# First tiles of a mixture of experts from two groups' counts, rows of 1216 bytes, and list scatters tied to other engines

## The chip, the cores and the metric

One core of one Trainium2 chip runs the whole kernel in one launch. The metric is device time in microseconds (us) of that core; the kernel before takes 544.88 us, the median of three runs (544.68 to 546.29).

## The reference, cut to what matters

```python
# x, ctx: (16, 128, 256).  16 batches of 128 tokens = 2048 tokens of 256 values
x = x + tanh(g_xattn) * xattn(ctx, ctx, layernorm(x))    # long convolution of k*v pairs, times q
x = x + tanh(g_ffn) * ffn(layernorm(x))

def ffn(x):                                   # 32 experts, 6 chosen for each token
    scores = sigmoid(xf @ w_router)           # (2048, 32)
    topk_idx = top 6 of (scores + corr_bias) within the 4 best of 8 expert groups
    combine[t, e] = scores[t, e] for the 6 chosen experts, else 0
    eo = (silu(xf @ gate_w[e]) * (xf @ up_w[e])) @ down_w[e]      # 256 -> 176 -> 256
    routed = sum over e of combine[:, e] * eo[e]
    shared = (silu(xf @ sh_gate_w) * (xf @ sh_up_w)) @ sh_down_w
    return routed + shared
```

## The kernel before, in words

The sixteen batches are worked in four groups of four (`GB = 4`, `NG = 4`). Each of the four groups goes through attention, layer norm, router, choice of experts and the shared expert; `group(g, attend, route)` exists once for each engine, and one call routes group g while it makes the attention products of group g + 1. The call for the last group (g = 3, `attend` False) has no attention products to make and builds the tile tables instead.

**Lists.** Every expert owns a list of 2048 rows in device memory (`expert_lists`), first filled with blank rows from SBUF. A row is `ROW = 289` floats: 256 normalised values, the token's number (`TOK_AT`), and its 32 router scores (`SCORE_AT:ROW`). Once VectorE has the slots of a group (`slots_ready`, L765), GpSimd sends 24 indirect DMAs (L395), one for each of 4 batches and 6 choices, each with 128 rows, at most `AHEAD = 6` of them unlanded. After 24 it waits until all have landed and raises `payload_free` (L400). SBUF holds the rows of two groups: `payload` for the even groups and `payload_2` for the odd ones.

**Tiles.** A tile is 128 rows of one expert's list. SyncE loads it (L313), TensorE transposes it (`xT`, L1196), multiplies it with the gate and up weights (`gate_up`, L1207), transposes the hidden values (`hT`, L1217) and multiplies with the down weights (`down`, L1226). VectorE copies x out (L973), picks the weight of each row (`pick`, L978 to L985) and multiplies up with silu (L991). ScalarE does the silu (L554), a copy (L561) and the scaled copy of y (L569) into one of 16 buffers. GpSimd adds y to `token_sums` with an indirect DMA (`add_tile`, L410); an add waits until the add two tiles before has landed, and its first one comes, in GpSimd's program, behind all 96 list scatters. The first program order on TensorE is xT(t), gate_up(t - 1), hT(t - 2), down(t - 3). There are 96 sure tiles and then blocks of four as the counts need; this input takes 108.

**The early table.** The first `NA = 16` tiles are full ones whose rows are known before the last group is routed. `describe_known` makes their table from `count_a`, the counts of the first `KNOWN = 12` batches (three groups), over the first `EA = 18` experts. VectorE copies the counts at group 2 (L757); the table is ready at L877 (`tables_a_ready`). The other tiles come from the whole counts (`describe_tiles`), ready at L951 (`tables_ready`). SyncE loads tiles into the four blocks of `payload`, `NX = 4` tiles ahead, so it first waits for `payload_free` to reach 4: the scatters of groups 0 to 2, of which groups 0 and 2 read `payload`.

**Weights.** The arena in SBUF holds all expert weights in the tile phase, and before that the attention's buffers; an expert's weights can be loaded once what lies there is dead. Up weights of the 14 first experts come early (L255 on SyncE). Behind `pairs_summed` 8, SyncE issues the down weights of experts 0 to 17 and the up weights of 14 to 17; ScalarE issues the up weights of 18 to 31 in one DMA after the scores of group 3, and behind `tables_ready` the down weights of 18 to 31 in two. TensorE waits for ScalarE's three DMAs (`last_in`) before tile 16.

**The end.** When all adds have landed, SyncE reads the two copies of `token_sums` back (L342), VectorE adds them to x (L1013, L1015) and the result is stored.

Of the kernel before, what the change touches and what calls it, by code (L numbers as in the profile page):

```python
# [9 lines left out]
GB = 4  # L10
# [17 lines left out]
ROW = L + 1 + E  # L28
TOK_AT, SCORE_AT = L, L + 1
# [30 lines left out]
assert ROUTER_AT + KC * E <= ARENA  # L60
# [3 lines left out]
WD_LAST = (X2T_AT - WD_AT) // WD_E // 2 * 2  # L64
assert WD_AT <= TMP_AT
# [13 lines left out]
assert TE_AT + NTILES <= WORK and NX <= GB  # L79

# [6 lines left out]
KNOWN = (NG - 1) * GB  # L87
EA = WD_MID
# [3 lines left out]
def build(nc, x, ctx_t, toeplitz, g_xattn, g_ffn, skip_d, w_router, corr_bias,  # L92
# [10 lines left out]
    with ctx:  # L103
# [18 lines left out]
        y_rows = sb("y_rows", [P, 3, L])  # L122
# [115 lines left out]
        y_at = [(y_rows, i * L) for i in range(3)] + [(blank, 0)]  # L238
        y_at += [(b, i * L) for b in (q_sb, shgu_sb, shd_sb) for i in range(4)]
        y_row = lambda t: win(*y_at[t % YR], [[1, L]])  # L240
        pick_w = lambda t: win(work, TW_AT + t % NPICK, [[1, 1]])
# [31 lines left out]
        def _(sp):  # L273
# [34 lines left out]
            def load_tile(t):  # L308
# [4 lines left out]
                sp.dma_start(payload[:, t % NX, :], lists[bass.ds(first, P), :]).then_inc(t_loaded[t % NX], 16)  # L313
# [38 lines left out]
        def _(pool):  # L352
# [25 lines left out]
            link(nc.gpsimd.tensor_scalar(tok_id[:, :], win(lane_dump, 0, [[0, B]]), float(B), None, ALU.mult))  # L378
            link(nc.gpsimd.tensor_tensor(tok_id[:, :], tok_id[:, :], iota_e[:, 0:B], ALU.add))
# [51 lines left out]
        def _(act):  # L431
# [18 lines left out]
            def group(g, attend, route):  # L450
# [51 lines left out]
                if route:  # L502
# [17 lines left out]
                    nc.scalar.activation(pay[g % 2][:, :, SCORE_AT:ROW], win(bank[4], 0, [[E, GB], [1, E]]),  # L520
                                         ACT.Sigmoid).then_inc(scores_ready, 1)
# [775 lines left out]
```

## Time and profile before

| what | value |
|---|---|
| median of three runs | 544.88 us |
| profiled execution: its own time, its span | 550.49 us, 548.6 us |
| TensorE busy, of the span | 445.5 us (81%) |
| VectorE, ScalarE, GpSimd busy | 312.8, 203.9, 288.6 us |
| mean granted TensorE clock | 0.903 of full speed |
| DMA traffic | 85.38 MB |

The span is the part that the profiler shows; 1.9 us of the execution's own time lie around it. Start times are in us from the span's start. "Busy" adds up instructions, so it says nothing of what the end waited for: that is read from the chain of waits and from the order of time. A releaser named "issue", "remote" or "unknown queue" is time for which the trace has no cause.

### The profile page before, as it was taken

Reading aid. Unit: us, or ns where it says so; the run is one execution under the profiler, and the core shown is the slowest. Engines: PE = TensorE matmul, PEld = TensorE weight load, DVE = VectorE, ACT = ScalarE, POOL = GpSimd, SP = SyncE. Lnnn points to the kernel's source line nnn. Section 1 sums busy time; section 2 is a strip of 40 time slices with the busy share of each in tenths; the row PEclk is TensorE's granted clock in tenths of the full one; section 3 lists DMA queues with packets and bytes.
Section 4 is the critical chain, followed back from the end, with each engine's and each line's share of the span. In section 5 each row is a group of like instructions: output and inputs, shape, how many; then the busy total and the mean of one; then the engine's idle time right before and its main releaser. Section 6 shows DMA issues by size and latency. Waiting matters only on the chain.

```text
span 548.6 us, 8656 instructions
## 1 busy us (share of the span) xinstructions
PE 445.5 (81%) x2114; PEld 334.4 (61%) x2114; DVE 312.8 (57%) x1163; ACT 203.9 (37%) x522; POOL 288.6 (53%) x224
## 2 busy tenths in 40 slices
PE   0924989798888668646999999999999999999900
PEld 0724767666766456424777777777777777777700
DVE  3999999859968755303444444444444444444307
ACT  3531725533462322002444444444444444444400
POOL 2000038848884752771556566665656566656630
PEclk9985989989988959755999999999999999999965
DMA  7999302222221499983666666566656665666569
GB/s 260 357 302 404 156 32 84 97 87 101 90 98 55 146 257 340 357 292 106 108 116 107 118 110 121 108 118 106 121 108 118 107 121 106 119 108 122 67 145 351
DMA packets 56053, 85.38 MB, mean 156 GB/s; under 512 B 6492, under 2 KB 47676, under 8 KB 55740
## 3 DMA queue, kind: packets, MB, share of 16 engines
q1 hardware_dynamic: 33566, 46.68, 28.8%
q0 software_dynamic: 20160, 28.37, 26.7%
q10 hardware_dynamic: 2270, 9.68, 4.6%
q8 instruction: 23, 0.38, 0.3%
q14 instruction: 34, 0.28, 0.2%
HBM read 44.91 MB, written 39.80 MB: 154 GB/s over the span
## 4 chain that ended last, share of the span: by engine, by line
PE 61%; DVE 22%; issue 7%; DMA 4%; ACT 2%; another core or an unknown queue 2%; SPq 1%; POOL 1%; DVEq 0%; POOLq 0%; ACTq 0%
PE bank L1207 24%; PE bank L1226 17%; DVE arena L658 5%; PE bank L1196 5%; PE bank L1217 4%; PE bank L1069 3%; DVE arena L636 3%; PE bank L1090 3%; DVE arena L666 3%; DMA arena<-token_sums 2%; DVE arena L615 1%; DMA rows<-x 1%; PE bank L1079 1%; PE bank L1040 1%
## 5 line engine op out<-in xcount | busy, mean ns | idle before, releaser
L395 POOL DMA_INDIRECT expert_lists<-payload,slots x96 | 116.7, 1216 | 126.3 <-DVE slots L765 84.3
L1207 PE MATMUL bank<-wgu,work 128*128 x432 | 149.8, 470 | 6.8 <-issue 5.2
L1226 PE MATMUL bank<-wd,work 88*128 x432 | 111.9, 382 | 0.0
L991 DVE TENSOR_TENSOR work<-work,bank 128x176 f32<-128x176 f32 x108 | 36.4, 337 | 128.2 <-ACT work L554 113.6
L1207 PEld LDWEIGHTS bank<-wgu,work 128*128 128x128 f32 x432 | 75.2, 194 | 31.8 <-issue 9.5
L554 ACT ACTIVATE work<-bank 128x176 f32<-128x176 f32 x108 | 34.2, 317 | 125.5 <-PE bank L1207 96.9
L1226 PEld LDWEIGHTS bank<-wd,work 88*128 88x128 f32 x432 | 73.9, 191 | 6.2 <-issue 0.2
L973 DVE COPY work<-bank 128x256 f32<-128x256 f32 x108 | 45.8, 424 | 34.4 <-PE bank L1196 18.6
L410 POOL DMA_INDIRECT token_sums<-q_sb,dest x28 | 43.6, 1558 | 27.2 <-ACT q_sb L569 7.3
L410 POOL DMA_INDIRECT token_sums<-shgu_sb,dest x28 | 43.6, 1559 | 24.8 <-DMA token_sums<-shgu_sb,dest 6.8
L1217 PEld LDWEIGHTS bank<-ident,work 128*88 128x88 f32 x216 | 26.5, 123 | 37.7 <-issue 18.8
L410 POOL DMA_INDIRECT token_sums<-shd_sb,dest x24 | 37.4, 1558 | 22.2 <-DVE work L985 7.7
L410 POOL DMA_INDIRECT token_sums<-y_rows,dest x21 | 32.8, 1561 | 29.7 <-ACT y_rows L569 15.3
L1217 PE MATMUL bank<-ident,work 128*88 128x128 f32 x216 | 41.8, 275 | 6.6 <-DVE work L991 6.6
L1040 PE MATMUL bank<-arena 128*128 128x288 f32 x128 | 45.8, 442 | 1.5 <-DVE arena L643 1.0
L1069 PE MATMUL bank<-shgu_sb,arena 128*128 128x352 f32 x128 | 46.5, 512 | 0.0
L658 DVE TENSOR_TENSOR arena<-arena,q_sb 128x448 f32<-128x448 f32 (+7 forms) x120 | 45.4, 454 | 0.0
L1196 PE MATMUL bank<-ident,payload 128*128 128x128 f32 x216 | 42.8, 280 | 0.7 <-issue 0.7
L561 ACT COPY work<-bank 88x256 f32<-88x256 f32 x108 | 39.7, 367 | 0.1
L1196 PEld LDWEIGHTS bank<-ident,payload 128*128 128x128 f32 x216 | 31.3, 146 | 12.6 <-issue 2.1
L457 ACT COPY arena<-bank 128x288 f32<-128x288 f32 x64 | 25.3, 399 | 26.7 <-PE bank L1041 23.4
L1069 PEld LDWEIGHTS bank<-shgu_sb,arena 128*128 128x128 f32 x128 | 26.2, 216 | 12.5 <-issue 4.0
(170 smaller groups left out, 570.1 us busy)
## 6 DMA issues: line engine op xcount, KB each, us to landing
payload<-expert_lists SPq DMA_DIRECT2D x108, 144.5 KB
wgu<-w_gu SPq DMA_DIRECT2D x1, 4928.0 KB, 19.1
wgu<-w_gu ACTq DMA_DIRECT2D x1, 4928.0 KB
expert_lists<-blank SPq DMA_DIRECT2D x1, 4768.5 KB, 25.4
arena<-token_sums SPq DMA_DIRECT2D x8, 512.0 KB, 7.3
wd<-w_down SPq DMA_DIRECT2D x1, 3168.0 KB
token_sums<-blank SPq DMA_DIRECT2D x1, 2304.0 KB, 28.9
arena<-toeplitz ACTq DMA_DIRECT2D x2, 1024.0 KB, 10.5
```

The source lines that it names most:

```text
L395: nc.gpsimd.indirect_dma_start(lists, bass.IndirectOffsetOnAxis(ap=slots[:, g % 2, b, k:k + 1], axis=0), pay[g % 2][:, b, :], None).then_i ...
L410: nc.gpsimd.indirect_dma_start(sums, bass.IndirectOffsetOnAxis(ap=dest[:, t % NPICK:t % NPICK + 1], axis=0), y_row(t), None, compute_op=AL ...
L561: nc.scalar.copy(win(work, HT_AT + t % 2 * L, [[1, L]], parts=MH), bank[4 + t % 2][0:MH, 0:L]).then_inc(t_hT_copied, 1)
L658: last = nc.vector.tensor_tensor(win(arena, Z_AT + z0, [[DH * DH, CELLS], [1, DH - d]]), y, win(q_sb, q_at + i0, [[DH, CELLS], [1, DH - d] ...
L973: nc.vector.tensor_copy(win(work, XT_AT + t % 2 * L, [[1, L]]), bank[t % 2][:, 0:L]).then_inc(t_x, 1)
L991: nc.vector.tensor_tensor(win(work, H_AT + t % 2 * M, [[1, M]]), win(work, SG_AT + t % 2 * M, [[1, M]]), bank[2 + t % 2][:, M:2 * M], ALU. ...
L1040: nc.tensor.matmul(y[:, 0:2 * CB], toe(h, 0), prods(s, hh, 0, 2), start=True, stop=False)
L1069: last = nc.tensor.matmul(bank[5 + half][:, 0:SHM], x2T(b, k), shgu_sb[:, k, half * SHM:(half + 1) * SHM], start=(k == 0), stop=(k == KC - 1))
L1196: last = nc.tensor.transpose(bank[t % 2][:, k * P:(k + 1) * P], payload[:, t % NX, k * P:(k + 1) * P], ident[:, :])
L1207: last = nc.tensor.matmul(bank[2 + t % 2][:, 0:2 * M], xT_half(t, k), wgu[:, bass.ds(e * WGU_E + k * 2 * M, 2 * M)], start=(k == 0), stop= ...
L1217: last = nc.tensor.transpose(bank[4 + t % 2][0:MH, c * P:(c + 1) * P], win(work, H_AT + t % 2 * M + c * MH, [[1, MH]]), ident[:, :])
L1226: last = nc.tensor.matmul(bank[6 + t % 2][:, 0:L], hT_half(t, c), wd[:, bass.ds(e * WD_E + c * L, L)], start=(c == 0), stop=(c == 1))
```

## The change

* `KNOWN` falls from 12 to 8 batches and `EA` from 18 to 14 experts; the early counts are taken at group 1 instead of group 2.
* A row grows from 289 to 304 floats (1156 to 1216 bytes); GpSimd sets the new tail to zero once.
* Tiles 0 to 7 (`IN_ARENA`) go to four blocks of their own in the arena, and SyncE loads them behind `payload_free` 3 (groups 0 and 1) and the early table; later tiles go to `payload` as before, behind `payload_free` 4.
* SyncE's late DMA is only the down weights of experts 0 to 13. All other weights come from ScalarE in 18 DMAs of two experts each: up weights in the last group's stage (six) and behind the steps of tiles 0 to 2 (three), down weights behind the steps of tiles 0 to 8.
* GpSimd waits before list scatters for counts of other engines. TensorE waits for 18 DMAs before tile 16.
* One y buffer moves from `y_rows` to `shgu_sb`; there are still 16.

```diff
-ROW = L + 1 + E
-TOK_AT, SCORE_AT = L, L + 1
+ROW = -(-(L + 1 + E) // 16) * 16
+TOK_AT, SCORE_AT, SCORE_END = L, L + 1, L + 1 + E
...
+TILES_AT = ROUTER_AT + KC * E
+assert TILES_AT + 4 * ROW <= ARENA
...
+WD_TILES = (ROUTER_AT - WD_AT) // WD_E // 2 * 2
+LATE = [n for n in range(EARLY, E, 2)]
...
+IN_ARENA = 2 * NX
-KNOWN = (NG - 1) * GB
-EA = WD_MID
+KNOWN = (NG - 2) * GB
+EA = EARLY
...
+        tile_rows = lambda t, at, n: (win(arena, TILES_AT + t % NX * ROW + at, [[1, n]]) if t < IN_ARENA
+                                      else payload[:, t % NX, at:at + n])
...
             sp.wait_ge(pairs_summed, 2 * NG)
-            load_down(sp, 0, WD_MID, late_in)
-            load_up(sp, EARLY, WD_MID, late_in)
+            load_down(sp, 0, EARLY, late_in)
+            sp.wait_ge(payload_free, NG - 1)
             sp.wait_ge(tables_a_ready, 1)
+            for t in range(IN_ARENA):
+                load_tile(t)
             sp.wait_ge(payload_free, NG)
-            for t in range(NX):
-                load_tile(t)
-            for t in range(NX, NA):
+            for t in range(IN_ARENA, NA):
                 load_tile(t)
...
+            for p in pay:
+                nc.gpsimd.memset(p[:, :, SCORE_END:ROW], 0.0)
...
+                        nth_of = b * TOPK + k
+                        if g == NG - 1 and 0 < nth_of < GB * TOPK // 2:
+                            pool.wait_ge(sh_h_ready, g * GB + 1 + nth_of // 3)
+                        elif g == NG - 2 and nth_of >= GB * TOPK // 2:
+                            pool.wait_ge(attn_ready, (g + 1) * 2 + 1)
+                            if nth_of >= GB * TOPK * 3 // 4:
+                                pool.wait_ge(x2T_ready, (g + 1) * 2 + 1)
+                        elif g < NG - 2 and nth_of >= GB * TOPK // 2:
+                            pool.wait_ge(conv_copied, (g + 2) * NH + 1 + (nth_of - GB * TOPK // 2) // 2)
+                        elif g == NG - 1 and nth_of:
+                            pool.wait_ge(t_xT, 1 + (nth_of - GB * TOPK // 2) // 2)
...
+                    if not attend:                                  # ACT, after the x2T copies
+                        act.wait_ge(pairs_summed, 2 * NG)
+                        load_up(act, EARLY, EARLY + 2, last_in)
...
                     if not attend:                                  # ACT, after the scores
-                        load_up(act, WD_MID, E, last_in)
+                        load_up(act, EARLY + 2, EARLY + 4, last_in)
...
+                        if not attend:                              # ACT, in the shared expert's loop over b
+                            load_up(act, EARLY + 4 + 2 * b, EARLY + 6 + 2 * b, last_in)
...
+            def late_weights(t):
+                if t < 3:
+                    n = EARLY + 12 + 2 * t
+                    load_up(act, n, n + 2, last_in)
+                if t < len(LATE):
+                    n = LATE[t]
+                    if n == WD_LAST:
+                        act.wait_ge(sh_stored, 16 * (B - GB))
+                        act.wait_ge(sh_added, GB)
+                    if n == WD_TILES:
+                        act.wait_ge(t_xT, IN_ARENA)
+                        act.wait_ge(t_picked, IN_ARENA)
+                    load_down(act, n, n + 2, last_in)
             act.wait_ge(tables_ready, 1)
-            load_down(act, WD_MID, WD_LAST, last_in)
-            act.wait_ge(sh_stored, 16 * (B - GB))
-            act.wait_ge(sh_added, GB)
-            load_down(act, WD_LAST, E, last_in)
...
+                if t < NA:                                          # ACT, last in tile_step(t)
+                    late_weights(t)
...
-                    if g == NG - 2:                                 # DVE and PE: the early counts
+                    if g == NG - 3:
...
-                    pe.wait_ge(last_in, 48)
+                    pe.wait_ge(last_in, 2 * len(LATE) * 16)
```

(The comments are added here. Where a kernel line read `payload[:, t % NX, ...]` for a tile, it now calls `tile_rows`, and `SCORE_AT:ROW` is now `SCORE_AT:SCORE_END`.)

## Rows read from the trace of the kernel before

**Rows 1.** The page's chain that ended last, share of the span by engine

```profile
PE 61%; DVE 22%; issue 7%; DMA 4%; ACT 2%; another core or an unknown queue 2%; SPq 1%; POOL 1%; DVEq 0%; POOLq 0%; ACTq 0%
```

**Rows 2.** The stretch of the tile loop: busy time by engine, clock, DMA share, GB/s

```profile
262.00:512.00 250.00, 250.00 (x1207) 185.28 (x1206) 115.60 (x505) 106.36 (x302) 155.68 (x101) 1.00 0.64 113
```

**Rows 3.** TensorE in order of time: start, length, line, operation, idle before

```profile
230.27 0.63 PE L1196 MATMUL bank<-ident,payload 128*128 128x128 f32 x2
235.68 2.71 PE L1207 MATMUL bank<-wgu,work 128*128 x4 [3.42 <-issue]
...
257.62 1.47 PE L1207 MATMUL bank<-wgu,work 128*128 x4
260.00 0.38 PE L1196 MATMUL bank<-ident,payload 128*128 128x128 f32 x2
262.72 1.35 PE L1207 MATMUL bank<-wgu,work 128*128 x4
...
516.53 1.35 PE L1207 MATMUL bank<-wgu,work 128*128 x4
```

**Rows 4.** The same table of busy times, three stretches around the tile loop's start

```profile
220.00:224.00 4.00, 3.59 (x19) 2.76 (x17) 2.08 (x11) 0.46 (x1) 3.06 (x4) 1.00 1.03 410
...
244.00:248.00 4.00, 0.00 (x0) 0.00 (x0) 0.00 (x0) 0.00 (x0) 3.08 (x4) 0.50 0.80 279
...
252.00:256.00 4.00, 3.45 (x8) 2.21 (x9) 1.80 (x8) 1.16 (x4) 0.00 (x0) 0.50 0.25 70
```

**Rows 5.** Who waited for whom, 226 to 262 us: total, times, longest

```profile
ACT work L554 <- issue: 22.3, 1, 22.3
```

**Rows 6.** GpSimd in order of time: last scatters of group 2, group 3's, first adds

```profile
206.81 0.96 POOL L395 DMA_INDIRECT expert_lists<-payload,slots  x1 [0.30 <-issue]
217.96 0.96 POOL L395 DMA_INDIRECT expert_lists<-payload,slots  x1 [10.19 <-issue]
247.04 0.96 POOL L395 DMA_INDIRECT expert_lists<-payload,slots  x1 [0.30 <-issue]
258.75 1.61 POOL L410 DMA_INDIRECT token_sums<-y_rows,dest  x1 [10.75 <-ACT y_rows L569]
```

**Rows 7.** GpSimd's read of the block count, just behind the last landing

```profile
L215 POOLq TENSOR_LOAD <-tile_code x1: 512/512/512, 252.4 to 252.4; - x1
```

**Rows 8.** GpSimd's adds, first and last of two stretches of 6 and 12

```profile
359.69 1.56 POOL L410 DMA_INDIRECT token_sums<-shgu_sb,dest  x1 [1.27 <-DMA token_sums<-q_sb,dest]
371.72 1.56 POOL L410 DMA_INDIRECT token_sums<-shd_sb,dest  x1 [1.00 <-DMA token_sums<-shgu_sb,dest]
...
489.26 1.56 POOL L410 DMA_INDIRECT token_sums<-shd_sb,dest  x1 [1.66 <-DMA token_sums<-shgu_sb,dest]
516.16 1.56 POOL L410 DMA_INDIRECT token_sums<-q_sb,dest  x1 [0.94 <-DMA token_sums<-q_sb,dest]
```

**Rows 9.** The chain's end in order of time: start, length, what

```profile
520.09 0.48 ACT shgu_sb L569
...
525.38 3.58 DMA token_sums<-shgu_sb,dest
```

**Rows 10.** VectorE in order of time, in the last group's stage

```profile
198.16 0.19 DVE L860 TENSOR_TENSOR taken_a<-arena 128x32 f32<-128x32 f32 x1 [1.82 <-remote]
```

**Rows 11.** DMA issues, 180 to 262 us: count, KB each

```profile
wgu<-w_gu ACTq DMA_DIRECT2D x1, 4928.0 KB
wd<-w_down SPq DMA_DIRECT2D x1, 3168.0 KB
wgu<-w_gu SPq DMA_DIRECT2D x1, 1408.0 KB
...
payload<-expert_lists SPq DMA_DIRECT2D x9, 144.5 KB
```

**Rows 12.** GpSimd in order of time, a long scatter of group 0

```profile
91.42 4.13 POOL L395 DMA_INDIRECT expert_lists<-payload,slots  x1 [0.30 <-issue]
```

**Rows 13.** ScalarE's issue of its up weights, in order of time

```profile
205.95 0.39 ACTq L255 DMA_DIRECT2D wgu<-w_gu  x1
```

More of the change, by code:

```diff
@@ L59 @@
 ROUTER_AT = SHOUT_AT + 2 * L
-assert ROUTER_AT + KC * E <= ARENA
+TILES_AT = ROUTER_AT + KC * E
+assert TILES_AT + 4 * ROW <= ARENA
 STATS_AT, MOMENTS_AT, NEWTON_AT = TMP_AT, TMP_AT + 6 * B, TMP_AT + 8 * B
@@ L121, in build @@
         payload_2 = sb("payload_2", [P, GB, ROW])
-        y_rows = sb("y_rows", [P, 3, L])
+        y_rows = sb("y_rows", [P, 2, L])
         blank = sb("blank", [P, ROW])
@@ L237, in build @@
         hT_half = lambda t, c: win(work, HT_AT + t % 2 * L + c * P, [[1, P]], parts=MH)
-        y_at = [(y_rows, i * L) for i in range(3)] + [(blank, 0)]
-        y_at += [(b, i * L) for b in (q_sb, shgu_sb, shd_sb) for i in range(4)]
+        y_at = [(y_rows, i * L) for i in range(2)] + [(blank, 0)]
+        y_at += [(b, i * L) for b, n in ((q_sb, 4), (shgu_sb, 5), (shd_sb, 4)) for i in range(n)]
         y_row = lambda t: win(*y_at[t % YR], [[1, L]])
+        tile_rows = lambda t, at, n: (win(arena, TILES_AT + t % NX * ROW + at, [[1, n]]) if t < IN_ARENA
+                                      else payload[:, t % NX, at:at + n])
         pick_w = lambda t: win(work, TW_AT + t % NPICK, [[1, 1]])
@@ L312, in load_tile @@
                 first = table_value(sp, tile_row, t, E * LIST)
-                sp.dma_start(payload[:, t % NX, :], lists[bass.ds(first, P), :]).then_inc(t_loaded[t % NX], 16)
+                sp.dma_start(tile_rows(t, 0, ROW), lists[bass.ds(first, P), :]).then_inc(t_loaded[t % NX], 16)
             def load_block(n):
@@ L519, in group @@
                     act.wait_ge(logits_ready, g + 1)
-                    nc.scalar.activation(pay[g % 2][:, :, SCORE_AT:ROW], win(bank[4], 0, [[E, GB], [1, E]]),
+                    nc.scalar.activation(pay[g % 2][:, :, SCORE_AT:SCORE_END], win(bank[4], 0, [[E, GB], [1, E]]),
                                          ACT.Sigmoid).then_inc(scores_ready, 1)
@@ L708, in flat @@
                         return win(arena, o, [[step, n]])
-                    scores = pay[g % 2][:, :, SCORE_AT:ROW]
+                    scores = pay[g % 2][:, :, SCORE_AT:SCORE_END]
                     sfc = tmp(GB, E)
@@ L977, in pick @@
                 mask = win(work, MASK_AT + t % 2 * E, [[1, E]])
-                nc.vector.scalar_tensor_tensor(mask, iota_e[:, :], tile_e[:, t:t + 1], payload[:, t % NX, SCORE_AT:ROW],
+                nc.vector.scalar_tensor_tensor(mask, iota_e[:, :], tile_e[:, t:t + 1], tile_rows(t, SCORE_AT, E),
                                                ALU.is_equal, ALU.mult).then_inc(t_masked, 1)
@@ L981, in pick @@
                     dve.wait_ge(t_added[t % NX], nth(t - NPICK))
-                nc.vector.tensor_scalar(dest[:, t % NPICK:t % NPICK + 1], payload[:, t % NX, TOK_AT:TOK_AT + 1],
+                nc.vector.tensor_scalar(dest[:, t % NPICK:t % NPICK + 1], tile_rows(t, TOK_AT, 1),
                                         tile_dump[:, t:t + 1], float(t % S * SUM_ROWS), ALU.max, ALU.add)
@@ L1148, in group @@
                                             start=False, stop=True)
-                    if g == NG - 2:
+                    if g == NG - 3:
                         for seen in range(KNOWN):
@@ L1196, in xT @@
                     last = nc.tensor.transpose(bank[t % 2][:, k * P:(k + 1) * P],
-                                               payload[:, t % NX, k * P:(k + 1) * P], ident[:, :])
+                                               tile_rows(t, k * P, P), ident[:, :])
                 last.then_inc(t_xT, 1)
@@ L1253, in _ @@
             pe.wait_ge(early_in, 16)
-            pe.wait_ge(late_in, 32)
+            pe.wait_ge(late_in, 16)
             last = last_block(pe)
```

## The prediction

> **What bounds the kernel now.** I read the chain first: TensorE holds 61% of the span and VectorE 22% [rows 1]. The order of time splits this in three. Up to about 188 us VectorE's attention arithmetic sets the pace. From 257.6 us the tile loop runs: between 262 and 512 us TensorE is busy without a gap at full clock [rows 2], and gate_up goes from tile 5 at 262.72 to tile 107 at 516.53 [rows 3], which is 253.81 / 102 = 2.488 us a tile. Between the two lies the loop's start, and there nothing is busy: the first transposes stand at 230.27 us, yet gate_up(3) comes at 257.62 [rows 3], and from 244 to 248 TensorE, VectorE and ScalarE do nothing while the DMA engines are 80% busy and the clock granted is half, 1.2 GHz [rows 4]. ScalarE starts silu(0) only at the end of a 22.3 us gap with no cause shown [rows 5]. The DMA share falls from 0.80 to 0.25 just as the work resumes [rows 4].
>
> A second chain runs beside TensorE and is hidden by its busy row: GpSimd's adds. Group 3's first list scatter is held until 217.96 by the landing of group 2's, the last goes at 247.04, and the first add at 258.75 [rows 6]. Where GpSimd didn't wait for y, 5 gaps take 12.03 us and 11 gaps 26.90 us [rows 8]: 38.93 / 16 = 2.433 us an add. So an add isn't made much faster than a tile (2.488), and adds that start late stay late. That is what I take to set the end after the change: last ScalarE copy at 520.09, last add landed 3.58 us after 525.38, and only then can the sums come back [rows 9].
>
> **The change, part by part.**
>
> *Number of tiles.* Routing the reference's inputs gives 107 tiles over all experts, so 108 run. Over two groups the first 14 experts have 6, 6 and 5 full tiles at experts 0, 1 and 11: 17, which fills the 16 early tiles. No blank tile is added, and the loop keeps 108 steps. Had it been fewer than 16, each missing one would cost 2.49 us.
>
> *Early counts.* Twelve small bf16 matmuls leave group 2 and eight join group 1, a few tenths of a us each way: 0.
>
> *Last group's stage, 188 to 230 us.* SyncE's burst at 188 us falls from 3168 + 1408 KB [rows 11] to 14/18 of 3168, which is 2464 KB, and ScalarE adds 704 KB pieces (two experts of the 14 that make 4928 KB). Just before the loop the DMA engines were full with 410 GB/s [rows 4]; fewer bytes are now in flight. VectorE had a 1.82 us hole at 198.16 on its path, waiting for its own semaphore [rows 10]. I take this 1.8 us as gone; bounds 0 (it isn't the bytes) and 3. The six issues on ScalarE cost 0.39 us each [rows 13] and lie beside TensorE's shared-expert matmuls: 0; without that cover 2.3 us.
>
> *Loop's start.* Tiles 0 to 3 load at the early table instead of behind group 2's landing, and nearly all of the queued weight bytes ahead of them are gone. Ten us of that landing wait [rows 6] fall out of the path of the loads. In an undisturbed start gate_up(0) would come 1.8 us earlier than 235.68, at 233.9. Behind it stand gate_up(1) and (2), each 2.71 us on the low clock [rows 3], five transposes of 0.63 and the first down: some 10 us, so gate_up(3) would come at about 244, 13.6 us earlier than 257.62. New load: three up and nine down pieces, 3 x 704 + 9 x 352 = 5280 KB, in the steps of tiles 0 to 8. At the 410 GB/s seen at best here [rows 4] that is 13 us of all DMA engines inside some 22 us, beside two scatters a tile. So I keep 2 us of the holes: 11.6 us earlier, the 1.8 us included. Bounds: 0 (the same holes, moved) and 15. Then xT(5), at 260.00 [rows 3], comes at 248.4.
>
> *Scatters of group 3.* Twelve are tied to the shared expert and the last twelve to t_xT 1 to 6, two a tile. Two take 2 x 1.26 us (pitch of the rows' 0.96 + 0.30 [rows 6]), so GpSimd keeps up, and the last ends at 248.4 + 2.5 = 250.9. Behind it in GpSimd's program stand the landing wait and every add. From the end of the last scatter before (248.0) to the count's read at 252.4 [rows 7] is 4.4 us; with 1.3 us for the read and the first issue, the first add comes at 256.6 instead of 258.75: 2.1 us earlier. Bounds: 10 later (TensorE starts no earlier and the ties hold) and 6 earlier.
>
> *The adds.* 11.6 - 2.1 = 9.5 us more backlog than before, about 4 tiles, within the 16 y buffers. The adds catch up at 2.488 - 2.433 = 0.055 us each, 107 x 0.055 = 5.9 us. Bounds: 0, and the whole 9.5 us.
>
> *Ties of groups 0 to 2.* The waits on convolution copies and on group 3's attention are, by the order of the program, met about when GpSimd gets to the second half of a group, since long scatters (4.13 us [rows 12] against 0.96) already hold it back beside VectorE's work. 0, bounds -2 (fewer collisions with VectorE's choice of experts) and +2 (a scatter held past the next group's need of `payload`).
>
> *Rows of 1216 bytes.* 5% more bytes in list loads and scatters, in a loop where the DMA share is 0.64 [rows 2]: 0, bounds -1 and +1. The Trainium skill, "DMA: Bandwidth & Descriptors", section "How a descriptor splits into AXI transactions", says that a transfer starting off a 256-byte boundary fetches unused bytes; 1216 is still no multiple of 256, so by it most rows stay misaligned, and no row of this trace prices it.
>
> *Late weights on ScalarE.* Two issues of about 0.4 us [rows 13] in steps 0 to 2, one in 3 to 8, beside 106.36 us busy in 250 [rows 2], 1.06 us in a tile of 2.49: hidden. TensorE's wait before tile 16 comes 40 us after the start, against 13 us of transfer: hidden; if not, a rival below.
>
> **Sum.** First add 2.1 us earlier, catching up 5.9: 8.0 us. The profiled execution took 550.49 us (548.6 span and 1.9 around it), 5.6 above the median of 544.88, so I subtract from each: 542.5 for it, 536.9 for the median; I say 537.
>
> **Rivals.**
>
> *A, the adds catch up (or GpSimd starts sooner).* If the landing wait is shorter in a quieter queue and an add takes 2.35 us when it never waits for y, the backlog is gone by the end, and TensorE's 11.6 to 15 us come through: 530 to 533. For it: the add's own 1.56 us leaves room in 2.433 [rows 8]. Against it: those are the gaps seen when landings alone held it. I say 532.
>
> *B, the ties and the adds eat all.* The loop starts earlier, the first add doesn't, and the pace is the tiles': no change, 544 to 546. For it: the first add came 11 us behind the last scatter [rows 6].
>
> *C, slower: the weights starve the loop.* 5280 KB in the steps 0 to 8 share the DMA engines with the tile loads, each of which needs its own 144.5 KB [rows 11] within a tile. The 80% busy stretch moved 279 GB/s [rows 4]; at this rate weights, twelve scatters and nine loads (5.4 + 1.9 + 1.4 MB) take 31 us, against 22 of nine tiles, and each queue gets only a share. If tiles 2 to 8 come at 5 us instead of 2.49, 17.5 us go, the twenty-fourth scatter waits with them, and the first add stands at about 268: 9 us later than before, 5 of them made up: 549. It decides from the point where a tile load takes over 2.5 us, three tiles in a row. The Trainium skill, "DMA: Bandwidth & Descriptors", section "Queues, rings and completion order", says that each DMA engine goes round the queues packet by packet; by this rule the tile loads' small packets stand one for one behind weight packets several times as long, and C's starved loads would be the rule. The trace agrees in so far as GpSimd's last scatters of group 2 took 10.19 us to land beside the weights [rows 6].
>
> **Chances.** Forecast (533 to 541) 0.48; A 0.24; B 0.15; C 0.13. About 0.3%, 1.6 us, is what a measurement tells here. B lies half within it and a quarter on each side, C is slower: faster 0.76, same 0.10, slower 0.14. The range that leaves out 2 in 10: 529 to 545. The forecast's own: 533 to 541.
>
> **What would show it.** Right: gate_up(3) near 246, silu(0) within 3 us of gate_up(0); the first add near 256 and at least 8 us behind the first y; adds released by DMA landings or by nothing nearly all through; a wider gap than 5 us between the last TensorE work and the last add. Wrong: adds waiting for y again by mid-loop (A); holes of TensorE in tiles 2 to 8 behind tile loads, or a wait before tile 16 (C); a first add at 258 or later (B).

## The result: 1.1% slower

| | before | after |
|---|---|---|
| median, same chip | 545.59 us (4 runs, 544.68 to 547.89) | 553.15 us (4 runs, 551.79 to 555.41) |
| profiled execution | 550.49 us, span 548.6 | 555.41 us, span 553.5 |
| gate_up(0), (3), (107) | 235.68, 257.62, 516.53 | 237.22, 244.86, 509.40 |
| group 3's scatters, first and last | 217.96, 247.04 | 214.76, 252.28 |
| adds 0, 4 and 107 | 258.75, 268.95, 525.38 | 261.07, 275.19, 530.25 |
| last ScalarE copy of y (the one at 520.09 in [rows 9] is the last but one) | 521.03 | 513.90 |

The ratio is 1.0112, with a 95% interval of 1.0069 to 1.0155; the quotient of the two medians, 1.0139, lies in it. In some executions of a kernel the chip is in a slower state: the ratios leave these out, the medians do not. TensorE's last gate_up comes 7.1 us earlier and the last add 4.9 us later. The span follows the add: 553.5 - 548.6 = 4.9.

After, the chain that ended last (answers to [rows 1]). VectorE fell from 22 to 14%, DMA rose from 4 to 11%:

```profile
PE 61%; DVE 14%; DMA 11%; issue 6%; ACT 3%; another core or an unknown queue 2%; POOL 1%; SPq 1%; DVEq 0%; POOLq 0%; ACTq 0%
```

After, TensorE in order of time (start, length, line, operation, idle before; answers to [rows 3]):

```profile
237.22 2.71 PE L1244 MATMUL bank<-wgu,work 128*128 x4 [1.26 <-DVE work L1010]
240.15 1.95 PE L1244 MATMUL bank<-wgu,work 128*128 x4
...
242.37 1.35 PE L1244 MATMUL bank<-wgu,work 128*128 x4
...
244.86 1.35 PE L1244 MATMUL bank<-wgu,work 128*128 x4
...
249.33 1.35 PE L1244 MATMUL bank<-wgu,work 128*128 x4
...
253.53 0.44 PE L1233 MATMUL bank<-ident,arena 128*128 128x128 f32 x2 [1.77 <-DMA arena<-expert_lists]
253.83 1.58 PE L1244 MATMUL bank<-wgu,work 128*128 x4
...
257.76 1.68 PE L1244 MATMUL bank<-wgu,work 128*128 x4
...
260.59 1.35 PE L1244 MATMUL bank<-wgu,work 128*128 x4
...
509.40 1.35 PE L1244 MATMUL bank<-wgu,work 128*128 x4
```

These are gate_up(0) to (7), and (107). gate_up(3) is 12.8 us earlier. Then come four tiles in 15.73 us instead of 4 x 2.488 = 9.95, one of them held openly by a tile load (the transpose at 253.53). So 5.8 us are lost again. From gate_up(7) on the pace is 2.488 once more: (509.40 - 260.59) / 100.

After, busy time by engine in two stretches (answers to [rows 4]; columns PE, PEld, DVE, ACT, POOL, granted clock, DMA share, GB/s):

```profile
244.00:248.00 4.00, 2.63 (x12) 1.47 (x10) 0.98 (x5) 0.68 (x3) 1.83 (x2) 1.00 0.99 322
252.00:256.00 4.00, 2.47 (x9) 1.75 (x10) 0.63 (x2) 0.92 (x3) 0.96 (x1) 0.88 0.95 337
```

Where before nothing ran on the three engines and the clock stood at 1.2 GHz (0.50), they work in the first stretch at 2.4 GHz (1.00). But from 252 to 256 us, where the DMA engines were 25% busy, they are now 95% busy.

After, GpSimd in order of time (answers to [rows 6, 8]):

```profile
214.76 0.96 POOL L414 DMA_INDIRECT expert_lists<-payload,slots  x1 [8.02 <-DVE arena L721]
...
236.31 0.96 POOL L414 DMA_INDIRECT expert_lists<-payload,slots  x1 [2.54 <-PE bank L1233]
...
252.28 0.96 POOL L414 DMA_INDIRECT expert_lists<-payload,slots  x1 [0.30 <-issue]
261.07 1.61 POOL L429 DMA_INDIRECT token_sums<-y_rows,dest  x1 [7.83 <-ACT q_sb L604]
262.99 1.58 POOL L429 DMA_INDIRECT token_sums<-y_rows,dest  x1 [0.30 <-issue]
269.72 1.56 POOL L429 DMA_INDIRECT token_sums<-blank,dest  x1 [5.14 <-DMA token_sums<-y_rows,dest]
272.25 1.56 POOL L429 DMA_INDIRECT token_sums<-q_sb,dest  x1 [0.97 <-DMA token_sums<-y_rows,dest]
275.19 1.56 POOL L429 DMA_INDIRECT token_sums<-q_sb,dest  x1 [1.38 <-DMA token_sums<-blank,dest]
...
285.02 1.56 POOL L429 DMA_INDIRECT token_sums<-shgu_sb,dest  x1 [0.84 <-DMA token_sums<-q_sb,dest]
288.46 1.57 POOL L429 DMA_INDIRECT token_sums<-shgu_sb,dest  x1 [1.89 <-ACT shd_sb L604]
...
530.25 1.56 POOL L429 DMA_INDIRECT token_sums<-shgu_sb,dest  x1 [1.13 <-DMA token_sums<-shgu_sb,dest]
```

After, ScalarE's last copy of y (answers to [rows 9]):

```profile
513.90 0.47 ACT L604 ACTIVATE shgu_sb<-bank,work 128x256 f32<-128x256 f32 x1 [0.47 <-PE bank L1263]
```

Three readings. The tied scatters end at 253.24, 5.2 us later than before. The first add follows 7.83 us behind; its releaser is named as ScalarE's copy, but the first y was written at 247.91, so the landings of the scatters held it (the run with the landing wait moved, below, shows it: there the first add follows the last scatter within 0.3 us). And the last add starts 16.35 us behind the last y: the adds don't wait for tiles any more. Against before, the last add is later by +2.32 (first add), +3.92 (first four gaps: 14.12 us instead of 10.20) and -1.37 (103 gaps: 255.06 instead of 256.43) = +4.87 us.

### The profile page after: what moved, and what is told of

It reads as the page before. It is cut to its first block, busy times and chain, and to the rows that moved or that the text cites. A ratio compares the mean times of both kernels' runs of the same rounds, so it can differ in the third digit from the quotient of the medians.

```text
span 553.5 us, 8724 instructions
## 1 busy us (share of the span) xinstructions
PE 446.7 (81%) x2110; PEld 337.3 (61%) x2110; DVE 312.6 (56%) x1163; ACT 204.3 (37%) x522; POOL 289.2 (52%) x226
## 3 DMA queue, kind: packets, MB, share of 16 engines
q1 hardware_dynamic: 33118, 45.60, 27.2%
## 4 chain that ended last, share of the span: by engine, by line
PE 61%; DVE 14%; DMA 11%; issue 6%; ACT 3%; another core or an unknown queue 2%; POOL 1%; SPq 1%; DVEq 0%; POOLq 0%; ACTq 0%
PE bank L1244 20%; PE bank L1263 14%; PE bank L1106 6%; PE bank L1127 4%; PE bank L1233 4%; PE bank L1254 4%; DVE arena L695 4%; DMA token_sums<-shgu_sb,dest 4%; PE bank L1077 3%; DVE arena L703 2%; DMA arena<-token_sums 2%; PE bank L1078 2%; DMA arena<-expert_lists 2%; PE bank L1116 1%
## 5 line engine op out<-in xcount | busy, mean ns | idle before, releaser
L1244 PE MATMUL bank<-wgu,work 128*128 x432 | 148.1, 466 | 1.3 <-DVE work L1010 1.3
L429 POOL DMA_INDIRECT token_sums<-shgu_sb,dest x35 | 54.6, 1559 | 31.8 <-DMA token_sums<-shgu_sb,dest 10.7
L1106 PE MATMUL bank<-shgu_sb,arena 128*128 128x352 f32 x128 | 48.3, 527 | 0.0
L1233 PE MATMUL bank<-ident,payload 128*128 128x128 f32 x200 | 38.3, 272 | 0.0
L1233 PEld LDWEIGHTS bank<-ident,payload 128*128 128x128 f32 x200 | 28.4, 142 | 10.1 <-DMA payload<-expert_lists 0.2
L1127 PE MATMUL bank<-shd_sb,arena 88*128 88x256 f32 x128 | 32.3, 397 | 1.3 <-issue 0.7
```

Source lines behind the costliest of these rows:

```text
L429: nc.gpsimd.indirect_dma_start(sums, bass.IndirectOffsetOnAxis(ap=dest[:, t % NPICK:t % NPICK + 1], axis=0), y_row(t), None, compute_op=AL ...
L1106: last = nc.tensor.matmul(bank[5 + half][:, 0:SHM], x2T(b, k), shgu_sb[:, k, half * SHM:(half + 1) * SHM], start=(k == 0), stop=(k == KC - 1))
L1127: last = nc.tensor.matmul(bank[4][:, 0:L], win(arena, HST_AT + c * P, [[1, P]], parts=MH), shd_sb[0:MH, c, :], start=(c == 0), stop=(c == 3))
L1233: last = nc.tensor.transpose(bank[t % 2][:, k * P:(k + 1) * P], tile_rows(t, k * P, P), ident[:, :])
L1244: last = nc.tensor.matmul(bank[2 + t % 2][:, 0:2 * M], xT_half(t, k), wgu[:, bass.ds(e * WGU_E + k * 2 * M, 2 * M)], start=(k == 0), stop= ...
```

## The experiments

Ratios are to the kernel before on the same chip, with the 95% interval. The edits are shortened. The chips were not alike. Before took 536.9 and 537.9 us on two of them and 545.6, 547.9, 549.1 and 549.6 on the other four. Before itself was traced on two of the slower ones only, so the chips can be compared by the traces of all kernels together. Between 95 and 260 us, VectorE, ScalarE and TensorE's matmuls have next to no waits that the profile can't explain ("issue" and "remote") on the two quick chips, at most 1.2 us in all; on the other four, ScalarE has 22 to 58 us of them, VectorE 7 to 32 and TensorE 2 to 22. The quoted expectations were written before this was known.

### On a quick chip: the parts one by one (before 536.9 us)

**Group 3's ties left out.**

```
-if g == NG - 1 and 0 < nth_of < GB * TOPK // 2: wait sh_h_ready
-elif g == NG - 1 and nth_of: wait t_xT
```

> The changed kernel without the waits of group 3's list scatters on sh_h_ready and t_xT; the ties of groups 0 to 2 stay. Theory T (the adds on GpSimd set the end, and they start late because group 3's scatters are tied to the tiles): 24 scatters from about 215 at 1.27 us each end at 245 instead of 253, the first add comes near 253 instead of 261, the pace stays about 2.48, and the time falls by 7 to 9 us to 544 to 546. Rival W (the weight pieces on ScalarE's queue beside tiles 0 to 8 slow landings and loads, whoever goes first): the first add comes earlier, but the scatters collide with the weights, landings get longer, and the time stays within 3 us of 553. Rival R (rows of 1216 bytes): no change, 553.

541.04 us, 1.0068 [1.0035, 1.0100]. Last scatter 238.28, first add 246.36, last y 493.75, last add 516.13. TensorE in order of time:

```profile
216.60 2.71 PE L1240 MATMUL bank<-wgu,work 128*128 x4 [1.53 <-DVE work L1006]
...
223.83 1.35 PE L1240 MATMUL bank<-wgu,work 128*128 x4
```

The loop starts without a standstill although GpSimd has no ties: 7.2 us from gate_up(0) to (3), against 21.9 in [rows 3]. Still the kernel is slower than before.

**Ties of groups 0 to 2 left out.**

```
-elif g == NG - 2 and nth_of >= 12: wait attn_ready, x2T_ready
-elif g < NG - 2 and nth_of >= 12: wait conv_copied
```

> The changed kernel without the waits of the scatters of groups 0 to 2; group 3's stay. Theory T: nothing, within 2 us of 553, because the trace of the changed kernel has these scatters at the same starts as before up to 0.3 us. Rival E (the early ties delay group 2's landing or the last group's stage): 2 us or more faster, with VectorE's choice of experts in groups 1 to 3 earlier.

539.12 us, 1.0054 [1.0024, 1.0085]. Last scatter 238.22, first add 245.78, last 515.19.

**Rows of 1156 bytes as before.**

```
-ROW = -(-(L + 1 + E) // 16) * 16
+ROW = L + 1 + E
```

> The changed kernel with rows of 289 floats (1156 bytes) again, nothing else. Theory T: within 2 us of 553. Rival R (longer rows cost DMA time in scatters, loads and landings): 3 us or more faster, with the DMA share of the tile loop down from 0.65 and the pace of the adds below 2.47.

539.96 us, 1.0049 [1.0017, 1.0082]. Last scatter 240.25, first add 248.44, last 514.63. Neither the early ties nor the longer rows show: three kernels with different parts of the change taken out agree within their intervals. The whole change wasn't timed on this chip, so that is as far as it goes.

**Landing wait moved.** All ties are kept. Group 3's scatters are waited for behind the fourth add and no longer ahead of the first.

```
-for landed in scattered: pool.wait_ge(...); pool.sem_inc(payload_free)
+if g < NG - 1: scatters_landed(g)
...
+if t == 4: scatters_landed(NG - 1)     # in the loop of adds
```

> The changed kernel, ties kept, with GpSimd's wait for the landing of group 3's scatters (and its signal to SyncE) moved from ahead of the first add to behind the fourth. Theory T: the first add comes right behind the last scatter, near 255 instead of 261, and the time falls by 4 to 6 us to 547 to 549. Rival W: the first adds start at 255 but land as slowly as the weights let them (6 to 8 us for each pair), the fifth add comes near 270 to 275 as it does now (275.19), and the time falls by less than 2 us.

534.23 us, 0.9957 [0.9939, 0.9976]: faster than before, and 1% below its three neighbours, although it keeps everything that each of them leaves out. Last scatter 239.67, first add 240.95, fifth 255.90, last 510.15. Against those neighbours the first add is 4.8 to 7.5 us earlier and the last 4.5 to 6.0. So on this chip the adds' chain ends the changed kernel.

### The weights and a third sum (before 549.12 us)

**Before once more**, for its trace.

> The kernel before, unchanged, for a trace of the chip on which the three kernels beside it run. Theory T (GpSimd's adds set the end of the changed kernel): here the first add still follows the first y within 10 us, and the last add follows the last y within 6 us, on this chip too. The rival that the chips differ only by a factor would have every stage scaled alike.

550.75 us in one execution. gate_up(0) to (3) at 238.28, 244.57, 251.93, 256.66: the slow start is there again. ScalarE waits 23.4 us in one piece, named "remote". gate_up(0), whose result it needs, ends at 240.99, and ScalarE starts at 250.31: 9.3 us of the piece are without a cause. In the other trace of before it is 10.8 us (238.39 to 249.15).

**The changed kernel once more.**

> The changed kernel, unchanged, beside the kernel before on one chip. Both theories: slower than before by 0.3 to 1.2%. Theory T: the last gate_up comes 10 us or more earlier than in the kernel before, the first add not, and the last add stands more than 15 us behind the last y.

555.98 us, 1.0116 [1.0071, 1.0161]. gate_up(3) 244.11, last y 513.82. GpSimd in order of time:

```profile
252.29 0.96 POOL L414 DMA_INDIRECT expert_lists<-payload,slots  x1 [0.30 <-issue]
261.00 1.61 POOL L429 DMA_INDIRECT token_sums<-y_rows,dest  x1 [7.75 <-ACT q_sb L604]
...
267.63 1.56 POOL L429 DMA_INDIRECT token_sums<-blank,dest  x1 [3.12 <-DMA token_sums<-y_rows,dest]
...
528.85 1.56 POOL L429 DMA_INDIRECT token_sums<-shgu_sb,dest  x1 [0.82 <-DMA token_sums<-shgu_sb,dest]
```

**ScalarE's weights in bulk**, the ties kept: most in the stage, four experts at tile step 7, nothing in the steps 0 to 6.

```
-load_up / load_down of two experts behind each of the steps 0 to 8
+load_up(act, EARLY, E)               # behind the scores
+load_down(act, EARLY, WD_TILES)      # behind tables_ready
+if t == 7: load_down(act, WD_TILES, E)
```

> The changed kernel with ScalarE's weights in bulk, as before: the up weights of experts 14 to 31 in one DMA behind the scores, the down weights of 14 to 27 in two behind the tables, 28 to 31 at tile step 7. Ties, early tiles and rows stay. Theory T: TensorE's first tiles come later (3 to 10 us, since loads stand beside the bulk), which doesn't matter, and the time changes by the first add's time alone: -3 to +3 us. Rival W (the pieces beside tiles 0 to 8 slow the adds' landings): the first five adds come at 2.5 us each instead of 3.3 or more, and the time falls by 3 to 6 us.

550.96 us, 1.0048 [1.0017, 1.0079]. gate_up(3) is unchanged at 244.44. GpSimd:

```profile
252.36 0.96 POOL L414 DMA_INDIRECT expert_lists<-payload,slots  x1 [0.30 <-issue]
256.78 1.61 POOL L429 DMA_INDIRECT token_sums<-y_rows,dest  x1 [3.46 <-DVE work L1015]
...
261.39 1.56 POOL L429 DMA_INDIRECT token_sums<-blank,dest  x1 [1.11 <-DMA token_sums<-y_rows,dest]
...
270.41 1.56 POOL L429 DMA_INDIRECT token_sums<-q_sb,dest  x1 [5.43 <-DMA token_sums<-blank,dest]
```

The last scatter goes at the same time, and its landing wait falls from 7.75 to 3.46 us. The last add comes 4.3 us earlier (524.57). So the late pieces cost 4.2 us through the landing wait alone. By the Trainium skill, "DMA: Bandwidth & Descriptors", section "Queues, rings and completion order", a DMA engine goes round the queues that have work, packet by packet, which would make each packet of a scatter stand behind a weight packet. These two traces agree (7.75 and 3.46 us).

The first four gaps of the adds did not shrink to 2.5 us each as rival W has it: they take 13.6 us together, against 12.4 in the changed kernel beside it. 6.98 us of that is one gap, from the add at 263.43 to the one at 270.41, held by a landing. It stands beside the one late piece that is left, four experts issued at 261.55; the DMA share is 0.93 from 264 to 268 us.

**A third sum**: adds go in turn to three copies of `token_sums`, so an add waits for the one three tiles before.

```
-S = 2
+S = 3          # and one more add of 128x1024 per chunk at the end
```

> The changed kernel with three copies of token_sums instead of two (S = 3), so an add waits for the landing of the one three before it. It costs one more copy to blank, to read back (2 MB, some 5 us at the 9.84 us that two took) and to add. Theory T: the adds, free of the landing, go at about 2 us until they have caught up, the last add comes within 6 us of the last y, 15 us or more earlier than in the changed kernel, and the time falls by 8 to 13 us. Rival P (TensorE's tile loop or GpSimd's own issue time sets the end): the last add moves by less than 3 us and the time rises by 3 to 5.

548.92 us, 0.9989 [0.9962, 1.0016]. GpSimd, then ScalarE:

```profile
514.41 1.56 POOL L429 DMA_INDIRECT token_sums<-shgu_sb,dest  x1 [0.71 <-issue]
...
518.13 1.56 POOL L429 DMA_INDIRECT token_sums<-shgu_sb,dest  x1 [0.30 <-issue]
515.16 0.47 ACT L604 ACTIVATE shgu_sb<-bank,work 128x256 f32<-128x256 f32 x1 [0.47 <-PE bank L1264]
```

The adds have caught up with the tiles at 313 us (from there each waits for its y, 2.49 us apart); the last comes 10.7 us earlier, 3 us behind the last y. The kernel gains 7 us (555.98 to 548.92). From the last add to the end of the span it is 29.3 us instead of 23.5: reading and adding a third copy takes 5.8 us back. With the moved landing wait, this shows the bound: where TensorE runs ahead, the adds' own landings end the kernel.

### What the ties do (before 547.89 us)

**Group 3's ties left out, on a slow chip.** Same kernel as the first.

> Again the changed kernel without the waits of group 3's list scatters. In its first run TensorE's stages before the loop ran some 20 us earlier than on the chips of the two comparisons of the changed kernel, and the ties held nothing there (last scatter at 238.28 without them, 238.22 with them). Where TensorE opens the loop near 237 us, theory T expects the last scatter at 245 instead of 252, the first add 5 to 8 us earlier than 261, and a ratio to before of 0.995 to 1.002 instead of 1.012. Where it opens near 216 us, the ratio stays at 1.005 to 1.007. Rival W: 1.01 wherever it runs.

557.98 us, 1.0166 [1.0122, 1.0211]. First add 253.82, first four gaps 20.3 us, last add 533.12, later than with the ties on the two other slow chips (530.25 and 528.85). Theory T expected a ratio of 0.995 to 1.002 for a start like this one. The stretch 230 to 240 us, and VectorE's longest wait between 226 and 250:

```profile
230.00:240.00 10.00, 3.14 (x6) 1.63 (x6) 1.29 (x5) 0.00 (x0) 7.71 (x8) 0.50 0.38 140
```

```profile
DVE rows L724 <- remote: 10.9, 1, 10.9
```

The standstill is back: gate_up(0) at 236.84, (3) at 249.55, 12.7 us apart against 7.6 with the ties. DMA is only 38% busy in it, and GpSimd is busy 7.71 us of 10.

**Ties out and landing wait moved.** Both edits above.

> The changed kernel without group 3's ties and with the landing wait behind the fourth add. Theory T: the first add comes 12 to 15 us earlier than in the changed kernel, right behind the last scatter and near the first y, and adds no longer end much behind y: ratio to before 0.98 to 0.99. Rival W: the first pairs of adds land in 6 us beside the weight pieces, half of the gain is lost, 0.995.

559.91 us, 1.0239 [1.0197, 1.0281], where 0.98 to 0.99 was expected. Without the ties the moved wait gains nothing here: gate_up(3) comes at 255.55, and the first adds take 20.7 us for four gaps.

**The same with weights in bulk** (both edits above and the third).

> As the kernel beside it, and ScalarE's weights in bulk as before. Theory T with what the bulk run showed: scatters and first adds land without the late pieces beside them, 2 to 4 us better than the kernel beside it, ratio 0.975 to 0.985, unless TensorE's start is late behind the bulk (then equal). Rival: the bulk holds the tile loads so long that TensorE, which now sets the pace from the start, begins 5 us later: ratio 0.99.

558.56 us, from 547.77 to 565.20, with a ratio of 1.0050 [0.9995, 1.0104] that rests on two of its six executions: inconclusive, and I read nothing from its trace.

**A third sum on the kernel before.** `S = 3`, nothing else.

> The kernel before with three copies of token_sums. Theory T says that in the kernel before y and the adds start together (258.75 against 257.43 us) and run at the same pace, so that the third copy gains 1 us at most at the end and costs its blanking and some 5 us of reading back and adding: ratio 1.005 to 1.012. Rival: the landing bounds the kernel before as well: ratio below 0.998.

551.54 us, 1.0081 [1.0051, 1.0112]: slower. The last add comes at 519.77, behind a last y at 516.79, and the third copy costs more than that brings. A faster chain pays only where the adds are late.

### The ties on their own (before 549.64 us)

Still open was whether the ties start the loop earlier, or the weights and early tiles.

**Before with group 3's two ties.**

```
+if g == NG - 1 and 0 < nth_of < 12: pool.wait_ge(sh_h_ready, g * GB + 1 + nth_of // 3)
+elif g == NG - 1 and nth_of:        pool.wait_ge(t_xT, 1 + (nth_of - 12) // 2)
```

> The kernel before with group 3's ties alone (eleven scatters on sh_h_ready, twelve on t_xT), all else as before. Theory S (GpSimd's back-to-back scatters hold up the other engines; the weights don't): gate_up(3) comes 5 us or more earlier than 256 to 258, the unexplained waits of ScalarE near the first silu (18 to 23 us in three traces of the kernel before) fall below 8, and the adds start later than 258, so that the time rises by 0 to 6 us. Theory D (the full DMA engines cause them, since 12 MB of weights move in this stretch): gate_up(3) stays near 257 and the time rises by 3 to 8 us. On a chip without such waits: no earlier gate_up, same or slower.

551.16 us, 1.0026 [0.9993, 1.0059]. TensorE, gate_up(1) and (3), and GpSimd:

```profile
239.27 2.71 PE L1212 MATMUL bank<-wgu,work 128*128 x4 [1.24 <-issue]
...
245.82 1.45 PE L1212 MATMUL bank<-wgu,work 128*128 x4 [0.80 <-DVE work L978]
```

```profile
253.50 0.96 POOL L400 DMA_INDIRECT expert_lists<-payload,slots  x1 [0.30 <-issue]
259.78 1.61 POOL L415 DMA_INDIRECT token_sums<-y_rows,dest  x1 [5.33 <-issue]
```

The stretch 235 to 248 us, first of this kernel, then of before on its other trace:

```profile
235.00:248.00 13.00, 10.82 (x36) 6.28 (x34) 4.07 (x18) 2.53 (x8) 7.01 (x8) 0.73 0.83 252
```

```profile
235.00:248.00 13.00, 5.85 (x10) 2.81 (x10) 1.23 (x5) 0.00 (x0) 9.30 (x10) 0.50 0.84 282
```

The DMA share is the same (0.83 and 0.84), the tile loads still stand behind group 2's landing, and yet gate_up(3) comes 11 us earlier than in before (256.66 and 257.62). VectorE, ScalarE and TensorE work where they stood. ScalarE's wait ahead of its first silu is still 13.4 us long in the profile, not below 8 as theory S has it, but gate_up(0) ends at 237.20 and the silu starts at 240.17: the part without a cause is 3.0 us, against 10.8 and 9.3.

So the ties alone are enough to start the loop earlier. Two limits: the traces of before come from other slow chips than this one, and before with three sums, whose start is that of before, has gate_up(3) at 252.09, so that the gain is 6 to 12 us. The early tiles and the fewer bytes are not enough: with them and without the ties, gate_up(3) came at 249.55 and 255.55 (and at 257.85, below). The last scatter moves from about 247 to 253.50 and takes the gain away again.

**Landing wait moved and three sums**, ties kept.

> The changed kernel with the landing wait behind the fourth add and three copies of token_sums; ties kept. Theory T with S: TensorE starts early as in the changed kernel, the first add comes 4 to 6 us earlier than 261, the adds catch up, and the last comes within 6 us of the last y: a ratio of 0.990 to 0.998. If the third copy already let the adds catch up (0.9989), moving the wait brings nothing: 0.998 to 1.0.

548.31 us, 0.9974 [0.9947, 1.0002]. First add 257.77, last 519.98, last y 517.00.

**Landing wait moved, once more.**

> Again the changed kernel with its landing wait moved, ties kept (0.9957 beside 1.005 for two kernels that should equal the changed one). Theory T: the first add 4 to 8 us earlier than 261, ratio to before 4 to 7 us below the changed kernel's 1.0116: 0.999 to 1.005 where the engines have unexplained waits. Rival W: first pairs land slowly, 1.008 to 1.012.

552.53 us, 1.0055 [1.0022, 1.0088]. GpSimd:

```profile
254.93 0.96 POOL L419 DMA_INDIRECT expert_lists<-payload,slots  x1 [0.30 <-issue]
256.19 1.62 POOL L433 DMA_INDIRECT token_sums<-y_rows,dest  x1 [0.30 <-issue]
...
265.23 1.56 POOL L433 DMA_INDIRECT token_sums<-blank,dest  x1 [5.53 <-ACT q_sb L610]
...
275.21 1.56 POOL L433 DMA_INDIRECT token_sums<-q_sb,dest  x1 [5.98 <-DVE work L1028]
```

The first add is 4.9 us earlier than in the changed kernel, but the fifth comes at the same 275.2: the landings hold the later adds instead. The last add, at 530.09, is as late as in the changed kernel (530.25 and 528.85). The ratio is 0.6% below the changed kernel's, within the intervals, and this trace shows no gain at the end.

**All ties on the shared expert.** The last twelve scatters no longer wait for tiles; the landing wait is moved.

```
-elif g == NG - 1 and nth_of: pool.wait_ge(t_xT, ...)
+if g == NG - 1 and 0 < nth_of: pool.wait_ge(sh_h_ready, g * GB + 1 + nth_of // 6)
```

> The changed kernel with all 23 of group 3's ties on sh_h_ready, six scatters to each of the four steps, none on t_xT, and the landing wait behind the fourth add. Theory S: pauses in the last group's stage are enough, only the last six scatters run together; TensorE's gate_up(3) within 3 us of 244, the last scatter near 237 instead of 252, the adds start with y and keep up: ratio 0.985 to 0.992. If the loop's start itself needs GpSimd's pauses, gate_up(3) comes at 250 or later, and the ratio is 1.0 to 1.01.

559.53 us, 1.0182 [1.0135, 1.0228], slower than either theory has it. These ties held nothing: the scatters run from 214.16 to 243.18 without a pause, 1.26 us apart, so this is one more kernel without pauses. Three stretches, then the longest waits between 205 and 262 us:

```profile
225.00:230.00 5.00, 0.00 (x0) 0.00 (x0) 1.52 (x6) 0.00 (x0) 3.78 (x5) 0.70 0.31 125
230.00:235.00 5.00, 1.08 (x4) 0.61 (x4) 0.30 (x1) 0.00 (x0) 3.78 (x5) 0.50 0.31 125
...
245.00:250.00 5.00, 0.00 (x0) 0.00 (x0) 0.82 (x2) 0.00 (x0) 0.00 (x0) 0.50 0.02 8
```

```profile
DVE rows L732 <- remote: 17.9, 1, 17.9
ACT arena L489 <- remote: 16.2, 1, 16.2
```

gate_up(3) is at 257.85 again. At a DMA share of 0.31 and 125 GB/s the engines stand still beside a GpSimd that issues back to back, and go on standing behind its last scatter: it ends at 244.14, gate_up(0) comes at 250.24, and the DMA share is 0.02 in between. So full DMA engines aren't needed for the standstill.

### Fewer scatters in flight (before 537.89 us)

If the number in flight were what stops the others, fewer should help.

```
-AHEAD = 6
+AHEAD = 3      # the second kernel: 2
```

> The kernel before with AHEAD = 3 instead of 6: a scatter waits for the landing of the one three before it. Theory S, any pause: a scatter then comes every 1.4 to 1.5 us, with short pauses; the unexplained waits of the other engines shrink in all stages, slots of group 3 come before 205 instead of near 209, and the time falls by 3 us or more. If short pauses don't help: the scatters only get longer, the last of group 3 comes 4 to 8 us later and the time rises by 0 to 5 us.

> The kernel before with AHEAD = 2: a scatter every 2 us, with pauses of about 1 us, some 49 us for a group against 46 between two groups. Theory S, any pause: no unexplained wait over 3 us before the tile loop, slots of group 2 near 157 as on the chip that shows none, but group 3's scatters end 12 us or more later than 247, and the adds behind them end the kernel: 3 us faster to 6 slower. If pauses of that size don't help: 10 us or more slower.

558.0 us, 1.0368 [1.0297, 1.0440], and 580.75 us, 1.0806 [1.0712, 1.0901]. The first is 20 us slower where either theory allowed 5 at most. The last scatters come at 260.24 and 281.76, the last adds at 532.04 and 552.19. This was a quick chip, and VectorE, ScalarE and TensorE's matmuls have next to no unexplained waits in these two traces (0.2 us) (before has none from this chip), so nothing is learned of the cause of the standstill. Only the price is: GpSimd's chain pays for every landing that it waits for.

## Why the prediction was wrong

Two terms of the sum failed: when the adds start, and how much they catch up. Behind both stands "Late weights on ScalarE: hidden". That was reasoned for TensorE and ScalarE alone; what the pieces do to the landings that GpSimd waits for was put at nothing.

**"What bounds the kernel now": right.** The adds end the kernel, the last y comes earlier, and the last add does not follow. Three sums move it by 10.7 us, on before they are a loss.

**"Loop's start": right in size by luck, wrong in cause.** gate_up(3) was forecast 11.6 us earlier and came 12.8. But gate_up(0) came at 237.22 and not at 233.9, 3.3 us late, and from it to gate_up(3) it took 7.6 us and not the 12.1 of the forecast. The two errors cancel. The forecast kept gate_up(1) and (2) at 2.71 us on the low clock (and left out gate_up(0)'s own 2.71); they took 1.95 and 1.35, and the granted clock went from 0.50 to 1.00 between 240 and 244 us. As to the cause, I put the gain down to early tiles and fewer bytes ahead of them. The run with ties alone shows 6 to 12 us with neither. Behind gate_up(3), the holes kept at 2 us were 5.8 (tiles 3 to 7), rival C in small, but they didn't set the end.

**"Scatters of group 3": mis-sized, 4.4 us.** Forecast: last one ends at 250.9, landing wait and first issue 5.7, first add at 256.6. Measured: 253.24, 7.83 and 261.07. The landing wait of before was taken for a kernel with 25% DMA load at that place [rows 4]; now it is 95%. Bulk weights bring it to 3.46.

**"The adds": mis-sized, 8.5 us.** Two parts. The first four gaps cost 3.9 us more than before, one of them 6.73 us (262.99 to 269.72), held by a landing; I had no term for that. The same late pieces run beside it (DMA share 0.98 from 264 to 268 us), the one late piece of the bulk run has a gap of 6.98 beside it, and before with ties, which has no pieces there, takes 10.1 us for the four. And 103 gaps took 2.476 us each, not 2.433: the adds made up 1.4 us, not 5.9. The 16 gaps that I averaged [rows 8] held none of the long ones. Five of the 103 are 3.1 to 3.9 us (one stands above, 285.02 to 288.46), each followed by a short one of 1.86 to 1.88. These ten gaps take 27.2 us where 2.433 each would be 24.3: 2.9 of the 4.5 us that are missing. The other 93 take 2.450 each, which is the rest. The trace of before showed such gaps: from add 8 to 9 it is 4.05 us and from 16 to 17 4.10, and these two places have a gap of over 3 us in 17 and 16 of the 20 traces. Why there is not known. Sum of the errors: 4.4 + 8.5 = 12.9 us, from -8.0 to +4.9.

**"Last group's stage": the hole stayed, and another came.** VectorE's hole of 1.82 us [rows 10] was to go with the fewer bytes in flight. It is 1.81 in the changed kernel, and a second one of 3.92 us, which was 1.64 before (at 223.70), stands ahead of the loop:

```profile
196.60 0.19 DVE L897 TENSOR_TENSOR taken_a<-arena 128x32 f32<-128x32 f32 x1 [1.81 <-remote]
...
227.69 0.29 DVE L985 CAST tile_row<-bank 128x128 int32<-128x128 f32 x1 [3.92 <-remote]
```

**"Ties of groups 0 to 2", "Rows of 1216 bytes", "Number of tiles": as said**, nothing seen; 108 tiles in both.

**Rivals.** A is out: the last add starts 16.35 us behind the last y. B had the mechanism (the first add no earlier, and the pace no help) but not its size. Its reason was misread, though: in before the first add came 11 us behind the last scatter because it waited for the first y, written from 257.43 to 257.90. C named the cause, weights beside the loop, but priced it on TensorE; it acted on the scatters' and adds' landings.

**Open.** Why the engines stand still while GpSimd issues, on four chips of six. Shown is that it needs neither full DMA engines nor the late weights, and that it is shorter where GpSimd pauses for tiles. Loads of code are an obvious rival. The traces have two instruction queues, and these move nothing in the standstill of before (226 to 250 us) or in the later one of the ties on the shared expert (238 to 250), which speaks against it without ruling out other queues. The experiment that leaves group 3's scatters out was not run. A version that surely beats before everywhere was not found: the moved landing wait has 0.9957 on the quick chip and 1.0055 on a slow one, with three sums 0.9974 [0.9947, 1.0002] there.

## What to carry to other kernels

When a change lets the main loop start earlier, follow the slower chain beside it: what it loses at the start comes out at the end almost undiminished, as long as its own pace (2.476 us) is hardly better than the loop's (2.488). A small difference of two paces times a hundred steps is no estimate; take the mean over all steps that the chain held itself, the rare long ones and the short ones behind them too. And transfers moved under the loop cost the small landings beside them first: a wait for scatters went from 3.46 to 7.75 us.

## What the runs showed of the hardware

* The kernel before took 536.9 to 549.6 us on six chips. In the traces from the slower four, VectorE, ScalarE and TensorE have waits without a cause, many of them while GpSimd issues indirect DMAs 1.26 us apart (up to 17.9 us in one piece, partly at a DMA share of 0.31); those from the two quick ones have next to none.
* An indirect scatter of 128 rows mostly takes GpSimd 0.96 us to issue, whether the rows are 1156 or 1216 bytes long (4.13 at times [rows 12]); an accumulating one takes 1.56.
* Accumulating scatters with at most two in flight came 2.43 to 2.48 us apart, with at most three 1.86 us when nothing else held them (514.41, 516.27, 518.13), which is GpSimd's own 1.56 + 0.30.
